# Attention in 25 turns of six or seven key tiles: longer groups of sums, a ring of eight steps, the last two tiles of a group in halves

## The reference

```python
def _L1_attn_ref(x, Wq, bq, Wk, bk, Wv, bv):
    q = jnp.einsum('bsd,de->bse', x, Wq) + bq
    k = jnp.einsum('bsd,de->bse', x, Wk) + bk
    v = jnp.einsum('bsd,de->bse', x, Wv) + bv
    d = x.shape[-1]
    scores = jnp.einsum('bqd,bkd->bqk', q, k) / jnp.sqrt(jnp.asarray(d, x.dtype))
    attn = jax.nn.softmax(scores, axis=-1)
    out = jnp.einsum('bqk,bkd->bqd', attn, v)
    return out + x
...
t = t + _L1_attn_ref(_ln_t(t), L1_attn_Wq, L1_attn_bq, L1_attn_Wk, L1_attn_bk, L1_attn_Wv, L1_attn_bv)
t = t + _L1_ffn_ref(_ln_t(t), L1_ffn_gate_w, L1_ffn_gate_b, L1_ffn_weight1, L1_ffn_weight2)
```

## Time and profile before

| | us |
|---|---|
| median of three runs | 3238.11 |
| lowest and highest | 3237.19 and 3240.19 |
| the profiled execution | 3244.04 |
| span of the profiled execution | 3242.5 |
| TensorE busy | 2908.9 (90%) |
| VectorE busy | 2450.4 (76%) |
| ScalarE busy | 2201.5 (68%) |
| GpSimd busy | 615.8 (19%) |
| attention stretch, 1117.5 to 3131.5 | 2014 |

### The profile page before, as it was taken

How to read it: one execution, slowest core, us unless ns; L and a number is a source line. 1 busy time by engine, 2 the same in 40 slices (tenths; PEclk the granted TensorE clock), 3 DMA queues, 4 the chain that set the end, 5 groups by cost and what they waited for, 6 DMA issues and landing times.

```text
span 3242.5 us, 67211 instructions
## 1 busy us (share of the span) xinstructions
PE 2908.9 (90%) x23873; PEld 1228.6 (38%) x23873; DVE 2450.4 (76%) x3155; ACT 2201.5 (68%) x3837; POOL 615.8 (19%) x493
## 2 busy tenths in 40 slices
PE   3788888888886899999999999999999999999987
PEld 3444444444443333333333333333333333333336
DVE  6788888888873887787786886877887877778744
ACT  2477677677664477776776776776776777677762
POOL 0344444444440011010010110110100100101100
PEclk7899999999998899999999999999999999999997
DMA  3000000000005601101001011011010010110002
GB/s 86 1 16 15 15 15 15 15 15 15 15 16 203 172 1 21 21 1 22 15 8 22 1 21 22 1 21 22 1 21 9 14 21 2 21 21 1 1 1 81
DMA packets 93908, 81.62 MB, mean 25 GB/s; under 512 B 62452, under 2 KB 83541, under 8 KB 92629
## 3 DMA queue, kind: packets, MB, share of 16 engines
q1 hardware_dynamic: 92085, 78.26, 9.3%
q10 hardware_dynamic: 1568, 0.04, 0.0%
HBM read 39.57 MB, written 32.11 MB: 22 GB/s over the span
## 4 chain that ended last, share of the span: by engine, by line
PE 62%; issue 13%; DVE 10%; POOL 6%; ACT 6%; DMA 2%; ACTq 1%; POOLq 0%; SPq 0%; DVEq 0%
PE ps L1661 19%; PE ps L1638 17%; PE ps L1608 16%; DVE arena L1212 5%; POOL arena L543 3%; PE ps L1671 2%; POOL arena L549 2%; ACT arena L698 1%; ACT L724 1%; PE ps L1488 1%; DMA arena<-in_x 1%; POOL arena L559 1%; DVE arena L1053 1%; PE ps L1720 1%; PE ps L1620 1%
## 5 line engine op out<-in xcount | busy, mean ns | idle before, releaser
L1212 DVE TENSOR_REDUCE arena<-ps 128x2 f32<-128x896 f32 (+1 forms) x1408 | 1483.1, 1082 | 432.2 <-PE ps L1608 420.6
L835 ACT ACTIVATE arena<-ps 128x512 f32<-128x512 f32 (+1 forms) x2464 | 1375.8, 595 | 520.5 <-PE ps L1638 508.1
L1638 PE MATMUL ps<-arena 97*128 97x512 f16 (+1 forms) x2800 | 895.0, 360 | 24.6 <-issue 20.0
L1608 PE MATMUL ps<-arena 96*128 96x448 f16 x2800 | 775.1, 360 | 35.8 <-DVE arena L1212 27.0
L1661 PE MATMUL ps<-arena 128*32 128x512 f32 (+1 forms) x6176 | 685.3, 522 | 17.6 <-DVE arena L1234 17.0
L1638 PEld LDWEIGHTS ps<-arena 97*128 97x128 f16 (+1 forms) x2800 | 254.4, 100 | 705.5 <-ACT arena L835 503.8
L1608 PEld LDWEIGHTS ps<-arena 96*128 96x128 f16 x2800 | 255.3, 99 | 326.4 <-DVE arena L1212 110.7
L608 POOL TENSOR_TENSOR tok<-arena,tok 128x128 f32 (+3 forms) x112 | 48.0, 429 | 1567.1 <-DVE arena L1234 1567.1
L549 POOL TENSOR_TENSOR arena<-arena 113x784 f32<-113x784 f32 x128 | 192.7, 1505 | 430.6 <-DVE arena L1062 430.6
L1661 PEld LDWEIGHTS ps<-arena 128*32 128x32 f32 x6176 | 132.0, 111 | 254.3 <-ACT arena L835 144.0
L543 POOL TENSOR_TENSOR arena<-arena 113x784 f32<-113x784 f32 x128 | 192.5, 1504 | 129.7 <-DVE arena L1053 129.7
(11 more groups left out here) (181 smaller groups left out, 2701.8 us busy)
## 6 DMA issues: line engine op xcount, KB each, us to landing
arena<-qk_scratch SPq DMA_DIRECT2D x96, 196.0 KB, 4.2
qk_scratch<-arena SPq DMA_DIRECT2D x16, 448.0 KB, 4.8
arena<-ximg SPq DMA_DIRECT2D x16, 400.0 KB, 7.0
arena<-in_x SPq DMA_DIRECT2D x4, 1568.0 KB, 8.5
xa_scratch<-arena SPq DMA_DIRECT2D x32, 196.0 KB, 1.9
res_scratch<-arena SPq DMA_DIRECT2D x32, 196.0 KB, 2.1
arena<-xa_scratch SPq DMA_DIRECT2D x4, 1568.0 KB, 8.5
arena<-res_scratch SPq DMA_DIRECT2D x4, 1568.0 KB, 12.9
```

What stands on the lines that cost most here:

```text
L835: act.activation(pk[0:rows, x % DEPTH, QC * m:QC * m + n], ps[0:rows, w % SB, 0:n], ACT.Exp, scale=float(C) ** -0.5).then_inc(att["exp"], 1)
L1212: dve.tensor_reduce(mxp[0:rows, p, 2 * u:2 * u + k], ps[0:rows, at_:at_ + k, 0:KN], AX_X, ALU.max)\
L1608: last = pe.matmul(ps[0:rows, MB + 2 * (j % 2) + n % 2, 0:KN], q2[p][0:96, T * t:T * t + rows], k2[p][0:96, KN * m:KN * m + KN], start=Tru ...
L1638: last = pe.matmul(ps[0:rows, bank, at_ % QC:at_ % QC + chunk_cols(c)], k2[p][0:97, T * t:T * t + rows], q2[p][0:97, QC * c:QC * c + chunk ...
```

## The change

The 80 steps of an image are put into 25 **turns**. A chunk of 13 steps makes turns of three, three, three and four steps, with six, six, six and seven scores; the last chunk is one turn. A turn issues its scores at numbered places and, at the places that `PLACES` names, a pair of key products before a score (or after the last). Then it issues all sums of the turn before as one group. Of six tiles, the first four go to the four column tiles, and each of the last two is cut into two halves of 256 columns (`parts = 2`), so that the four halves fill the four column tiles. In a turn of seven tiles the fifth and sixth stay whole and go to column tiles 0 and 1, and the seventh is cut in quarters as before.

The row of maxima goes between the first and the second step of that group, in the turn after the one with its last reductions. The output products stand at place 2 or 3 of the turn after the one that holds the chunk's last sums. `DEPTH` becomes 8, since the exponentials of more than two turns are alive; the ring takes more room, so some arrays move in the arena. The number of products for scores, keys and outputs, of exponentials and of reductions is the same.

```diff
-DEPTH = 4
-LAG = 2
+DEPTH = 8
...
+        turns = []
+        for c in range(NQ):
+            n = last_of[c] - first_of[c] + 1
+            starts = [*range(0, n - 1, 3)]
+            ends = starts[1:] + [n]
+            turns += [list(range(first_of[c] + i, first_of[c] + j)) for i, j in zip(starts, ends)]
+        NTURN = len(turns)
+        scores_of = [sum(k for x in xs for _, _, k, _ in steps2[x][2]) for xs in turns]
+
+        def chunk_ended(k):
+
+            x = turns[k % NTURN][-1]
+            return [(c, int(k < 0)) for c in range(NQ) if last_of[c] == x]
+
+        OUT_PLACE = {6: 3, 7: 3, 4: 2}
...
+        def jobs_until(k):
+
+            return -(-NJ * sum(scores_of[:k]) // sum(scores_of))
+
+        PLACES = {(6, 3): (1, 3, 5), (6, 4): (0, 2, 4, 6), (7, 3): (1, 3, 5), (7, 4): (1, 3, 5, 7)}
...
-                for t, at_ in tiles:
-
-                    parts = 4 if t == NT - 1 and n == QC else 1
+                full = c < NQ - 1
+                turn_of = [k for k in turns if x in k][0]
+                alone = full and (len(turn_of) == 3 and x == turn_of[2])
+                for i, (t, at_) in enumerate(tiles):
+
+                    parts = 4 if t == NT - 1 and full else 2 if alone else 1
                     w = n // parts
                     for h in range(parts):
-                        g = h if parts > 1 else t % 4
+                        g = h if parts == 4 else 2 * i + h if parts == 2 else (2 * (turn_of.index(x) % 2) + i if full else t % 4)
...
             def image_steps(b, p, first=False, last=False):
...
+                for k in range(NTURN):
+                    mine = [(x, i) for x in turns[k] for i in range(len(units[x]))]
+                    for place in range(scores_of[k] + 1):
+                        if place == OUT_PLACE[scores_of[k]]:
+                            for c, late in chunk_ended(k - 2):
+                                if not (late and first):
+                                    out_values(b - late, c)
+                        for j, ahead, u in jobs_at(k, place, last):
+                            produce(b + ahead, (p + ahead) % 2, u, j, b * NJ + AHEAD + j - 1)
+                        if place < scores_of[k]:
+                            second_scores(b, p, *mine[place], last)
+                    for i, x in enumerate(turns[k - 1]):
+                        if k:
+                            key_sums(b, p, x, last)
+                        elif not first:
+                            key_sums(b - 1, 1 - p, x)
+                        if i == 0 and k in row_turn and not (last and row_turn[k] == NQ):
+                            c = row_turn[k]
```

More of the change, by code:

```diff
@@ L338, in last_pair, with jobs_at @@
             return (min(NK * 4 * (c + 1), FP) - 1) // 2
[L340 to L347, removed]
+        def jobs_until(k):
+            return -(-NJ * sum(scores_of[:k]) // sum(scores_of))
+        PLACES = {(6, 3): (1, 3, 5), (6, 4): (0, 2, 4, 6), (7, 3): (1, 3, 5), (7, 4): (1, 3, 5, 7)}
+        def jobs_at(k, place, last):
+            first, n = jobs_until(k), jobs_until(k + 1) - jobs_until(k)
+            at_ = PLACES[scores_of[k], n] if k < NTURN - 1 else (2,) * n
+            return [(first + i, *jobs[first + i]) for i in range(n) if at_[i] == place and not (last and jobs[first + i][0])]
         MB = 4
@@ L648, in _ @@
             image_steps(B - 1, 1)
[L649 to L652, removed]
+            tokens(B - 1, 1, NQ - 2)
+            tokens(B - 1, 1, NQ - 1)
             pool.wait_ge(att["var"], B + 1)
@@ L853, in _ @@
             image_steps(B - 1, 1, last=True)
[L854 to L857, removed]
+            sums_copy(B - 1, NQ - 1)
             def token_columns(o, n, gg):
@@ L1260, in image_steps @@
             def image_steps(b, p, first=False, last=False):
[L1261 to L1272, removed]
-                    if x == LN_AT + 9:
-                        variance_slot(b)
+                for k in range(NTURN):
+                    for place in range(scores_of[k] + 1):
+                        if place == OUT_PLACE[scores_of[k]]:
+                            for c, late in chunk_ended(k - 2):
+                                if not (late and first):
+                                    weighted(b - late, (p + late) % 2, c)
+                        for j, ahead, u in jobs_at(k, place, last):
+                            consume(b + ahead, (p + ahead) % 2, u, j, b * NJ + AHEAD + j + 1)
+                            if j == LN_AT:
+                                sum_slot(b)
+                            if j == LN_AT + 1:
+                                mean_slot(b)
+                            if j == LN_AT + 9:
+                                square_sum(b)
+                            if j == LN_AT + 10:
+                                variance_slot(b)
             for u in range(AHEAD):
@@ L1284, in _ @@
             image_steps(B - 1, 1, last=True)
-            for x in range(LAG + 3):
-                for c, late in chunks_at(over_at, x):
-                    if late:
-                        weighted(B - 1, 1, c)
+            weighted(B - 1, 1, NQ - 2)
+            weighted(B - 1, 1, NQ - 1)
             def token_columns(n):
@@ new lines, in image_steps @@
+            def image_steps(b, p, first=False, last=False):
+                for k in range(NTURN):
+                    mine = [(x, i) for x in turns[k] for i in range(len(units[x]))]
+                    for place in range(scores_of[k] + 1):
+                        if place == OUT_PLACE[scores_of[k]]:
+                            for c, late in chunk_ended(k - 2):
+                                if not (late and first):
+                                    out_values(b - late, c)
+                        for j, ahead, u in jobs_at(k, place, last):
+                            produce(b + ahead, (p + ahead) % 2, u, j, b * NJ + AHEAD + j - 1)
[8 more added lines that the diff above has]
+                            c = row_turn[k]
+                            bank, done = turn(row_unit[c], 1 if isinstance(b, int) and b == 0 else NUNIT, SB)
+                            if c == NQ:
+                                max_row(b + 1, 1 - p, 0, bank, 1 + b * NUNIT + done)
+                            else:
+                                max_row(b, p, c, bank, 1 + b * NUNIT + done)
```

138 lines of the change are left out of this document (48 added, 90 removed).

## The result

The changed kernel takes **3161.97 us** (median; 3153.07 to 3166.55) where the kernel before took 3238.24 in the same comparison: a ratio of 0.9749, 95% interval 0.9734 to 0.9764. The forecast was 3207, its range began at 3180. The direction was right, the gain 2.5 times as large as forecast: 76 us in place of 31. The profiled executions differ by more, 3151.5 against 3242.5 us of span.

The account below looks back on a forecast made before the run. TensorE was taken to bound the attention stretch. Terms -1.7, -0.9, +0.7 and -0.3 gave -2.2 us an image; 16 images plus 1 made -34, rounded to -31: median 3207 us from 3238.11, range 3180 to 3243.

Parts of the forecast that it names:

- The change of size before the 64-row score: Score of the last key tile, now behind a 128-row score: one more size change, 0.12 us, six times an image, +0.7.
- Parts 1 to 3: Per image: sums of full chunks -1.7 us, rows of maxima moved into groups -0.9, score of last key tile +0.7.
- 25-product group: Group of 25 products of 64 columns: 0.90 us, 0.15 of it fixed, read as a cost per group, not per product.
- part 4: TensorE's waits per image: 4.8 us before, 4.5 after, so -0.3, with -1.3 for waits on L1234 contained in it.
- The walks of the two turns: Ring waits stepped through: six scores with three pairs lose 0.11 us a turn, seven scores with four pairs 0.13.
- two round additions: Waits after, per image: 0.8 us for layer-norm sums on VectorE and small reductions of maxima, 0.8 for smaller waits.
- the estimate of the old waits: TensorE's waits in the kernel before: 1.3 + 2.7 + 0.8 for smaller ones, put at 4.8 us an image.
- my rounding down: The total gain of -34 us was rounded towards the unknowns to -31.
- The second, the row that comes too late: Chunk's first score blocked until ScalarE copies the row: 0.45 us five times an image, 3243; 0.9 each, 3279; chance 0.07.
- The first, consumers as the bound: VectorE runs dry in groups and is late after: 5.0 us an image of new waits, 3287 us; chance 0.08.
- The third: Column tiles don't stay filled: halves run one after another, a six-tile group costs 1.85 us, 3297 us; chance 0.03.
- Fewer waits than walked: TensorE's waits come out smaller than the walk through the turns gave: 3180 to 3197 us; chance 0.15.

Follow-up runs that it names:

- Padding: Kernel before, with eight more products of 512 columns in the last score of each image in front of the loop's jump: 3221.70 us, ratio 0.9953.
- control: Kernel before, with the same eight extra products in the other image of the loop body, away from the jump: 3249.33 us, ratio 1.0034.
- the last experiment: Changed kernel, images written out, tiles 22 and 23 in halves, 18 pairs ahead, row of maxima issued before the group's first sums: 3090.21 us, ratio 0.9540.

## Why the prediction fell short

**Where it held.** The bound was TensorE. A full product per column tile, a half and a quarter cost 0.85, 0.43 and 0.21; the groups came out at 1.43 and 2.06 as worked out. The change of size before the 64-row score costs 0.09 and not 0.12. Parts 1 to 3 sum to -1.8 us an image before rounding; with that correction and 0.19 in place of 0.17 for a row in a six-tile group they are -1.9, 31 us in all. The rule of the Trainium skill ("TensorEngine Tiling (Array Packing)", Instruction Overhead) on an overhead of each matmul, weighed there against the 25-product group, would have left 7 us less, by the prediction's estimate; the halves' groups, 1.43 as worked out without it, show none of it.

**The term that was mis-sized: the waits, part 4.** It said 4.8 before, 4.5 after, -0.3 an image. For the two kernels without a loop, I added up how much longer each distance between starts is than the shortest tenth of its kind: 95 us before, 5.9 an image. After, it is 53, and 12 more for the row waits, which that sum doesn't see since nearly all such distances have them: 4.1 an image. So -1.8, 29 us in all; with the 31 of parts 1 to 3 that is 60 of the 63 us, and 3 are in neither count. The walks of the two turns shown above were right to 0.01 us. Wrong were the two round additions, 0.8 + 0.8 after: 3.3 us an image came of the walked 2.9 and these 1.6. That the turns have slack for VectorE's side work would explain it; no run tested it. Wrong was also the estimate of the old waits, 1.1 too small. Against that stands a wait that was not in the sum, that for the row's copy.

**The step that failed beside it: "The loop round stays at two images, so I leave the share of the 1.2 GHz level in the stretch (mean 0.98) as it is."** This put a term at nothing that was not nothing. The number of rounds stayed, but not what lay in front of the jump. Padding and control show that the stop at the head depends on it, and the versions without a loop price it: about 12 us by the medians, 24 in the profiled execution, where the clock fell once behind a head and not six times. Of the miss of 45 us about 12 are this, about 25 the waits and 3 my rounding down; the few that are left are within what the medians can tell.

**The rivals.** The second, the row that comes too late, did happen, at 0.2 us and not 0.45 or more: four chunk starts an image, about 12 us by the wait's own size and by the stretch of the last experiment. The walk counted only ScalarE's seven exponentials and the copy behind them; in fact the row's signal was the late one, 0.73 behind its products. The first, consumers as the bound, did not come: VectorE is busy in 78% of the stretch. The third is ruled out by the group of 1.43; its price of 3297 was also added up wrongly, for 7.6 us an image less the 31 gained is +90 on the kernel before, 3328. "Fewer waits than walked" was the nearest and still 18 us short, and the range held no case in which something outside the sum moved with it.

## What to carry to other kernels

When a stage is bound by TensorE in column tiles, count groups and idle column tiles first: each group costs a fixed 0.24 us here, and an idle half of the array costs as much as work. Look at what TensorE has queued when a loop jumps: a long group there covers part of the stop, a short one exposes it, and the clock can fall behind it. And put a small product on whose result another engine waits in front of the long ones, not among them.

## What the runs showed that I had not expected

- **The jump costs TensorE about 3.4 to 4.1 us** from the start of the last group to the first product of the next round, in both kernels; queued work covers it nearly one for one (0.36 us of sums: stops of 3.0 to 3.6; 2.06 us: 1.6 to 2.0; eight more products: 1.5 to 2.0). One version with a group of 1.65 us had stops of 2.8 to 3.3, about 1 us more than this sum gives; why was not settled.
- **The clock behind a stop.** After TensorE had stood idle for 2.8 to 3.6 us it was granted the 1.2 GHz level at 18 of 18 heads (three versions), for 3 to 14 us. After stops of 1.5 to 2.4 us it was so at 15 of 30 (five versions): once in the changed kernel, and at all six heads of the version without halves. Without a loop it did not happen in the stretch.
- **The signals of products came in the order of the instructions.** A row whose products are recorded from 1510.58 to 1510.97, on a column tile of its own, was signalled at 1511.70, when the two longer products issued ahead of it, on other column tiles, had ended; issued first, it was signalled 0.01 after its end. By these records the products overtake each other between column tiles and the signals do not. This rests on the one edit and the traces; no run varied the length of the products in front.
- **More work can be faster**: eight useless products in front of the jump took 16 us off, the same eight elsewhere added 11.
